# Turning the squared distances into weights: pairs of blocks with two exponentials and one subtraction

## The chip, the cores and the metric

The kernel runs on all 8 cores of one Trainium2 chip. Each core works alone on half of one batch element's queries (2048 of 4096 tokens) against all 4096 keys; the cores exchange nothing. The metric is the device time of the slowest core. Before the change it is 4728.23 us, the median of three runs (4728.14 to 4728.63).

## The reference, cut to what matters

One layer: a layer norm, attention with a kernel of inverse squared distance in place of softmax, a residual, then a second layer norm and a product with the signs of a weight.

```python
P = layernorm(x) @ W_in + b_in           # 16 heads, each Q, K, V, G of 64 columns
d2 = q2[..., :, None] + k2[..., None, :] - 2.0 * qk
W = power(EPS + sqrt(maximum(d2, 0)), -2)          # EPS = 1e-4
W = W / (EPS + sum(W, axis=-1, keepdims=True))
H = G * (W @ V)
x = x + H @ W_out + b_out
x = x + layernorm(x) @ sign(weight).T
```

The matrix W has 4096 x 2048 entries for each head and core; it is never stored, only computed in tiles and contracted with V at once. The power is computed from L = Ln(d2): with d = exp(L/2), (EPS + d)^-2 is close to exp(-L) * (1 - 2 EPS exp(-L/2)).

## The kernel before, in words

Every engine has its own list of steps, written by Python code in the order in which the helper `st` is called for that engine; each step waits for counts of semaphores and then adds to one. Nothing is reordered afterwards, so the order of the emitting code is the order of each engine's queue, and a waiting step holds back everything behind it on its engine. DMAs are issued by SyncE (big loads and stores) and by GpSimd (rows of one partition).

Stages: first layer norm and transposition into `XnT` (some 230 us), the projection of head 0, then the attention loop over 16 heads, then the output projection, the second layer norm and the last product.

The attention loop runs over 1024 regions, r = 0 to 1023: 16 heads, 4 blocks of 512 queries in each, 16 regions in each block. A region is 256 keys by 512 queries. The 64 regions of a head are called slots 0 to 63 below. For one region:

- `emit_S` (L478): two matmuls (512 columns each) write the squared distances to one of two PSUM tiles `pS`; they wait until region r-2 has left it.
- `emit_c12`: ScalarE computes `Lb` = Ln (L490) and `Eb` = Exp(-L/2 + ln 2 EPS) (L495).
- `emit_c3` (L500): VectorE adds the two, in float32, 128 x 1024.
- `emit_c4` (L508): ScalarE computes the weights `wb` = Exp(-(sum)) in bfloat16; four such tiles.
- `emit_A` (L521): two matmuls add weights times V to a PSUM bank `pA`; the 65th row collects the sum of the weights.

The loop writes, at step r: Ln and Exp of r, the addition of r, the distances of r+1, then the last Exp and the matmuls with V of r-1. After the 16th region of a block comes the epilogue (`emit_epilogue`): VectorE copies `pA` to `A_sb` (L534), GpSimd issues a DMA of its sum row (L540), ScalarE takes Ln and Exp of it (L543, L545), VectorE splits it into two bfloat16 rows (L548, L550), TensorE spreads them (L557, L561), and VectorE multiplies (L566 and L574 or L581).

Between these steps `splice` puts the projection of the next head, in 61 groups (the first empty), one after almost every slot: slots 2 to 5 Q, 6 to 13 K (eight matmuls of 512 columns each, L331, and a VectorE copy out of the single PSUM tile `pp`, L341 or L350), slots 14 to 47 V (eight matmuls of 64 columns, L362, a copy L369), 48 to 51 G (as Q, L374), and 52 to 63 the squared norms of K and Q. A group of this last kind, a row group below, is: VectorE squares 512 columns (`KQsq`, L388), TensorE sums over partitions with one matmul (L396), VectorE copies the row out (`k2row`, L400), GpSimd sends it by DMA into `Kaug` or `Qaug` (L405, L410). The first `emit_S` of a head waits for the last of these DMAs. The last head has no such groups. The weights of the next head are loaded and cast after slot 0 (`flush_w`, L312, L316).

Of the kernel before, what the change touches and what calls it, by code (L numbers as in the profile page):

```python
# [34 lines left out]
def build_nc():  # L35
# [448 lines left out]

    def emit_c12(r):
        ps = r % 2
        w = [(s_peS, 2 * r + 2)]
        if r >= 2:
            w.append((s_c3, r - 1))
        st("scalar", lambda e, ps=ps, r=r: e.activation(  # L490
            out=Lb[r % 2][:], in_=pS[ps][:], func=AF.Ln), waits=w, inc=s_c1)
        w = [(s_c1, r + 1)]
        if r >= 2:
            w.append((s_c4, r - 1))
        st("scalar", lambda e, r=r: e.activation(  # L495
            out=Eb[r % 2][:], in_=Lb[r % 2][:], func=AF.Exp, scale=-0.5, bias=LN2EPS),
           waits=w, inc=s_c2)

    def emit_c3(r):
        st("vector", lambda e, r=r: e.tensor_tensor(  # L500
            out=Eb[r % 2][:], in0=Lb[r % 2][:], in1=Eb[r % 2][:], op=ALU.add),
           waits=[(s_c2, r + 1)], inc=s_c3)

    def emit_c4(r):
        w = [(s_c3, r + 1)]
        if r >= 4:
            w.append((s_wcons, 2 * r - 6))
        st("scalar", lambda e, r=r, ws=r % 4: e.activation(  # L508
            out=wb[ws][:], in_=Eb[r % 2][:], func=AF.Exp, scale=-1.0),
           waits=w, inc=s_c4)  # L510
# [390 lines left out]
```

How the kernel before makes its waits and increments, by code:

```python
            def run(eng):  # L840
                for waits, fn, inc, inc_n in steps[name]:
                    for (sm, val) in waits:
                        if val > 0:
                            eng.wait_ge(sm.h, val)
                    inst = fn(eng)
                    if inc is not None:
                        inst.then_inc(inc.h, inc_n)
```

## Time and profile before

| what | value |
|---|---|
| median of three runs | 4728.23 us |
| the profiled execution, own time | 4748.2 us |
| its span (slowest core, first to last instruction) | 4746.6 us |
| spans of the eight cores | 4719.4 to 4746.6 us |
| mean granted TensorE clock, of full speed | 0.629 to 0.633 |
| ScalarE busy | 3168.7 us (67%) |
| TensorE matmul busy | 2870.4 us (60%) |
| VectorE busy | 2254.5 us (47%) |
| GpSimd busy | 145.7 us (3%) |
| attention loop, in the span | 373 to 4393 us |

Busy times are of one execution on its slowest core. The engines work side by side, so that their shares do not add up; what a stage costs is read from the work and the waits of that stage. A row of the order of time gives start, duration, engine, line, operation, tiles, and in brackets how long the engine stood idle before it and for whom. Granted clock 0.50 is 1.2 GHz and 1.00 is 2.4 GHz. Durations contain the latency of an instruction, so that two of one engine that do not wait for each other overlap a little; what one costs the engine is the distance of two starts.

### The profile page before, as it was taken

How to read it: one execution, taken by the hardware profiler on the slowest of the kernel's cores; microseconds unless marked ns; L12 is line 12 of the kernel's file. 1: busy time of each engine (PE TensorE's matmuls, PEld its weight loads, DVE VectorE, ACT ScalarE, POOL GpSimd, SP SyncE). 2: the span in 40 equal slices, each digit the busy share in tenths (PEclk: the TensorE clock that was granted, in tenths of full speed). 3: DMA queues.
4: the chain of work that ended last, by engine and by line, in shares of the span. 5: the costliest groups of instructions: out<-in, count | busy, mean ns of one | idle time of the engine just before them, and what ended most of it. 6: DMA issues, size and time to landing. Idle time of an engine off the chain costs nothing.

```text
span 4746.6 us, 50533 instructions; the slowest of 8 cores (4719.4 to 4746.6 us)
## 1 busy us (share of the span) xinstructions
PE 2870.4 (60%) x11472; PEld 1018.3 (21%) x11472; DVE 2254.5 (47%) x3142; ACT 3168.7 (67%) x3345; POOL 145.7 (3%) x300
## 2 busy tenths in 40 slices
PE   1146666666666576666666666666565766655626
PEld 0122222121212121222222121212121212211202
DVE  4524444545444454454544445454444544533254
ACT  2206868687868687777878686868686877888000
POOL 0000000000000000000000000000000000000000
PEclk9986565656566565656565656565665656555656
DMA  2200000000000000000000000000000000000301
GB/s 76 69 10 10 1 10 2 10 1 10 2 11 1 10 2 5 6 1 10 2 10 1 10 2 10 1 10 2 11 1 10 2 1 17 1 1 2 120 14 71
DMA packets 41423, 64.47 MB, mean 14 GB/s; under 512 B 12992, under 2 KB 29376, under 8 KB 40128
## 3 DMA queue, kind: packets, MB, share of 16 engines
q1 hardware_dynamic: 31680, 58.79, 3.9%
q0 software_dynamic: 9472, 2.45, 0.3%
q8 instruction: 123, 2.02, 0.2%
q14 instruction: 148, 1.21, 0.1%
HBM read 50.39 MB, written 8.39 MB: 12 GB/s over the span
## 4 chain that ended last, share of the span: by engine, by line
issue 29%; ACT 27%; PE 22%; DVE 14%; DMA 6%; ACTq 1%; DVEq 1%; SPq 0%; POOLq 0%
ACT Lb L490 14%; ACT wb L508 9%; PE pp L331 6%; PE pA L521 4%; PE pS L478 3%; DVE k2row L400 3%; PE pp L396 2%; DMA Wst<-w_in 2%; DMA rsrow<-A_sb 2%; DVE KQsq L388 2%; PE pS L815 1%; PE pS L663 1%; ACT Eb L495 1%; ACTq L844 1%; PE pp L362 1%
## 5 line engine op out<-in xcount | busy, mean ns | idle before, releaser
L500 DVE TENSOR_TENSOR Eb<-Lb,Eb 128x1024 f32<-128x1024 f32 x1024 | 1251.5, 1223 | 472.0 <-ACT Eb L495 415.8
L521 PE MATMUL pA<-wb,Vs 128*65 128x512 bf16 x2048 | 943.7, 558 | 790.9 <-ACT wb L508 785.0
L490 ACT ACTIVATE Lb<-pS 128x1024 f32<-128x1024 f32 x1024 | 1035.0, 1011 | 468.7 <-PE pS L478 466.3
L495 ACT ACTIVATE Eb<-Lb 128x1024 f32<-128x1024 f32 x1024 | 1082.1, 1057 | 154.7 <-ACT Lb L490 6.9
L508 ACT ACTIVATE wb<-Eb 128x1024 bf16<-128x1024 f32 x1024 | 1065.3, 1040 | 141.4 <-DVE Eb L500 140.6
L478 PE MATMUL pS<-Qaug,Kaug 66*128 66x512 bf16 x2048 | 944.0, 560 | 57.2 <-POOLq L416 56.8
L521 PEld LDWEIGHTS pA<-wb,Vs 128*65 128x65 bf16 x2048 | 257.5, 127 | 1541.8 <-issue 1529.3
L331 PE MATMUL pp<-XnT,Wbf 128*64 128x512 bf16 x2048 | 543.6, 413 | 40.3 <-DVE Wbf L316 25.0
L369 DVE CAST Vs<-pp 128x64 bf16<-128x64 f32 x512 | 114.7, 224 | 557.0 <-PE pp L362 556.9
L362 PEld LDWEIGHTS pp<-Wbf,XnT 128*128 128x128 bf16 x4096 | 281.5, 129 | 257.5 <-issue 254.7
L362 PE MATMUL pp<-Wbf,XnT 128*128 128x64 bf16 x4096 | 313.5, 240 | 16.4 <-DVE Vs L369 15.4
L331 PEld LDWEIGHTS pp<-XnT,Wbf 128*64 128x64 bf16 x2048 | 219.2, 117 | 334.4 <-issue 193.2
L557 PE MATMUL pA<-rnhl,ones_rowb 1*64 1x512 bf16 x64 | 38.4, 600 | 400.5 <-DVE rnhl L550 400.5
L478 PEld LDWEIGHTS pS<-Qaug,Kaug 66*128 66x128 bf16 x2048 | 177.6, 121 | 311.0 <-issue 308.8
L543 ACT ACTIVATE rlrow<-rsrow 1x512 f32<-1x512 f32 x64 | 40.2, 628 | 285.2 <-DMA rsrow<-A_sb 285.2
L400 DVE CAST k2row<-pp 1x512 bf16<-1x512 f32 x192 | 130.4, 679 | 190.4 <-PE pp L396 190.4
L350 DVE TENSOR_SCALAR Kaug<-pp,bin_sb 64x512 bf16<-64x512 f32 x128 | 95.5, 746 | 167.3 <-PE pp L331 167.3
L396 PE MATMUL pp<-KQsq,ones_col 64*1 64x512 bf16 x128 | 70.8, 553 | 138.9 <-DVE KQsq L388 138.9
L224 PE MATMUL pT<-c_identb,xnf 128*128 128x128 bf16 x256 | 32.4, 306 | 199.4 <-DVE xnf L212 199.4
L548 DVE CAST rnhl<-rnrow 1x512 bf16<-1x512 f32 x64 | 26.6, 416 | 243.2 <-ACT rnrow L545 243.2
L540 POOL DMA_DIRECT2D rsrow<-A_sb x64 | 31.2, 488 | 2857.5 <-DVE A_sb L534 2807.0
L188 ACT ACTIVATE sqscr<-xst 128x1024 f32<-128x1024 f32 x32 | 33.8, 1056 | 126.7 <-DVE lnrows L185 126.7
(85 smaller groups left out, 1256.2 us busy)
## 6 DMA issues: line engine op xcount, KB each, us to landing
xst<-x SPq DMA_DIRECT2D x32, 512.0 KB, 3.7
Wst<-w_in SPq DMA_DIRECT2D x128, 128.0 KB, 2.1
XT<-xT SPq DMA_DIRECT2D x8, 1024.0 KB, 17.2
...
xst<-w_out SPq DMA_DIRECT2D x8, 512.0 KB, 4.6
xst<-w_ffn SPq DMA_DIRECT2D x8, 512.0 KB, 3.5
Kaug<-k2row POOLq DMA_DIRECT2D x128, 1.0 KB, 1.5
...
```

The lines of the kernel that those rows point to most:

```text
L331: return e.matmul(pp[0:64, :], Wbf[hb][:, c * 256 + cols0:c * 256 + cols0 + 64], XnT[:, c * SLEN + n * 512:c * SLEN + (n + 1) * 512], star ...
L350: return e.tensor_scalar(out=Kaug[hb][0:64, n * 512:(n + 1) * 512], in0=pp[0:64, :], scalar1=bin_sb[64:128, 2 * h:2 * h + 1], scalar2=None ...
L362: return e.matmul(pp[0:128, 0:64], XnT[:, c * SLEN + t * 128:c * SLEN + (t + 1) * 128], Wbf[hb][:, c * 256 + 128:c * 256 + 192], start=(c ...
L369: return e.tensor_copy(out=Vs[hb][:, t * 65:t * 65 + 64], in_=pp[0:128, 0:64])
L396: return e.matmul(pp[0:1, :], scol[0:64, :], KQsq[sl][:], start=True, stop=True)
L400: return e.tensor_copy(out=k2row[sl][:], in_=pp[0:1, :])
L478: st("tensor", lambda e, hb=hb, qc=qc, stile=stile, ps=ps, k=k: e.matmul(pS[ps][:, k * 512:(k + 1) * 512], Kaug[hb][:, stile * 128:(stile ...
L490: st("scalar", lambda e, ps=ps, r=r: e.activation(out=Lb[r % 2][:], in_=pS[ps][:], func=AF.Ln), waits=w, inc=s_c1)
L495: st("scalar", lambda e, r=r: e.activation(out=Eb[r % 2][:], in_=Lb[r % 2][:], func=AF.Exp, scale=-0.5, bias=LN2EPS), waits=w, inc=s_c2)
L500: st("vector", lambda e, r=r: e.tensor_tensor(out=Eb[r % 2][:], in0=Lb[r % 2][:], in1=Eb[r % 2][:], op=ALU.add), waits=[(s_c2, r + 1)], in ...
L508: st("scalar", lambda e, r=r, ws=r % 4: e.activation(out=wb[ws][:], in_=Eb[r % 2][:], func=AF.Exp, scale=-1.0), waits=w, inc=s_c4)
L521: st("tensor", lambda e, hb=hb, stile=stile, ws=r % 4, k=k, bk=bk: e.matmul(pAb[bk][0:65, :], Vs[hb][:, stile * 65:stile * 65 + 65], wb[ws ...
```

## The change

Two regions, 2s and 2s+1, are now handled together after their logarithms. The logarithm stays one instruction for each region, and writes one half of a tile `Lb` of 2048 columns. After the second, ScalarE computes `Ea` = Exp(-L) in float32 and `Ebc` = Exp(-1.5 L + ln 2 EPS) in bfloat16, 2048 columns each (`emit_c24`), and VectorE subtracts them into `wb`, bfloat16, 128 x 2048 (`emit_c3`). So three exponential-type passes over each element stay three, but the last step before the matmuls is now on VectorE, and the addition and last exponential are gone. There is one `Ea` and one `Ebc`, and two `wb` of double size: the first exponential of a pair waits for the subtraction of the pair before. The matmuls with V of a pair come together, four in a row, one step later, and the epilogue behind them. Larger tiles need room: the tiles `xst` and `sqscr` are given back after the first layer norm, and the later stages get their own (`wst2`, `wst3`, `sq2`); the first loads of the output weight now wait for the last distance matmul, those of the last weight for the end of the output projection.

```diff
-    Lb = [salloc(f"Lb{i}", [128, 1024], F32, side="right") for i in range(2)]
-    Eb = [salloc(f"Eb{i}", [128, 1024], F32, side="right") for i in range(2)]
-    wb = [salloc(f"wb{i}", [128, 1024], BF16, side="right") for i in range(4)]
+    Lb = [salloc(f"Lb{i}", [128, 2048], F32, side="right") for i in range(2)]
+    Ea = salloc("Ea0", [128, 2048], F32, side="right")
+    Ebc = salloc("Ebc", [128, 2048], BF16, side="right")
+    wb = [salloc(f"wb{i}", [128, 2048], BF16, side="right") for i in range(2)]
...
+    def emit_c1(r):
         ps = r % 2
+        st("scalar", lambda e, ps=ps, sb=(r // 2) % 2, half=r % 2: e.activation(
+            out=Lb[sb][:, half * 1024:half * 1024 + 1024],
+            in_=pS[ps][:], func=AF.Ln),
+           waits=[(s_peS, 2 * r + 2)], inc=s_c1)
+
+    def emit_c24(s):
+        st("scalar", lambda e, s=s: e.activation(
+            out=Ea[:], in_=Lb[s % 2][:], func=AF.Exp, scale=-1.0),
+           waits=[(s_c1, 2 * s + 2), (s_c3, s)], inc=s_c2)
+        st("scalar", lambda e, s=s: e.activation(
+            out=Ebc[:], in_=Lb[s % 2][:], func=AF.Exp, scale=-1.5, bias=LN2EPS),
+           waits=[], inc=s_c2)
+
+    def emit_c3(s):
+        st("vector", lambda e, s=s: e.tensor_tensor(
+            out=wb[s % 2][:], in0=Ea[:], in1=Ebc[:], op=ALU.subtract),
+           waits=[(s_c2, 2 * s + 2), (s_wcons, max(0, 4 * s - 4))], inc=s_c3)
...
-            w = [(s_c4, r + 1)]
+            w = [(s_c3, s + 1)]
...
-        emit_c12(r)
-        emit_c3(r)
+        emit_c1(r)
+        if r % 2 == 1:
+            emit_c24(r // 2)
+            emit_c3(r // 2)
         nxt_head_start = (r + 1) % (NQC * NREG) == 0
         if r + 1 < NTOT and not nxt_head_start:
             emit_S(r + 1)
-        if r >= 1:
-            emit_c4(r - 1)
-            emit_A(r - 1)
-            hh, qq, gg = rinfo(r - 1)
+        if r % 2 == 0 and r >= 2:
+            s = r // 2
+            emit_A(2 * s - 2)
+            emit_A(2 * s - 1)
+            hh, qq, gg = rinfo(2 * s - 1)
             if gg == NREG - 1:
-                emit_epilogue(r - 1)
+                emit_epilogue(2 * s - 1)
...
-           waits=[(s_xfree[sl], NST // 2), (s_wo, max(0, s_wo.n - 1))], inc=s_xld[sl], inc_n=16)
+           waits=[(s_peS, s_peS.n), (s_wo, max(0, s_wo.n - 1))], inc=s_xld[sl], inc_n=16)
...
-           waits=[(s_sg, max(0, s_sg.n - 1)), (s_wo, WO_DONE)], inc=s_xld[sl], inc_n=16)
+           waits=[(s_sg, max(0, s_sg.n - 1)), (s_x1, X1_DONE)], inc=s_xld[sl], inc_n=16)
```

ScalarE's queue around an epilogue (rlrow and rnrow), in the kernel before:

```order
L490 ACTIVATE Lb0<-pS0 128x1024
L495 ACTIVATE Eb0<-Lb0 128x1024
L508 ACTIVATE wb3<-Eb1 128x1024
L543 ACTIVATE rlrow<-rsrow 1x512
L545 ACTIVATE rnrow<-rlrow 1x512
L490 ACTIVATE Lb1<-pS1 128x1024
L495 ACTIVATE Eb1<-Lb1 128x1024
L508 ACTIVATE wb0<-Eb0 128x1024
L490 ACTIVATE Lb0<-pS0 128x1024
```

and in the changed kernel:

```order
L488 ACTIVATE Lb1<-pS0 128x1024
L488 ACTIVATE Lb1<-pS1 128x1024
L494 ACTIVATE Ea0<-Lb1 128x2048
L497 ACTIVATE Ebc<-Lb1 128x2048
L488 ACTIVATE Lb0<-pS0 128x1024
L538 ACTIVATE rlrow<-rsrow 1x512
L540 ACTIVATE rnrow<-rlrow 1x512
L488 ACTIVATE Lb0<-pS1 128x1024
L494 ACTIVATE Ea0<-Lb0 128x2048
L497 ACTIVATE Ebc<-Lb0 128x2048
```

Before, the exponential that feeds the block's last matmuls stands directly ahead of rlrow; now only a logarithm stands between the last pair's exponentials and rlrow.

TensorE's queue where the row groups are spliced in (pS are distances, pA the matmuls with V, pp a row group's matmul), before:

```order
L396 MATMUL pp<-KQsq1,ones_col 1x512
L478 MATMUL pS0<-Qaug0,Kaug0 128x512 x2
L521 MATMUL pA2<-wb0,Vs0 65x512 x2
L396 MATMUL pp<-KQsq0,ones_col 1x512
L478 MATMUL pS1<-Qaug0,Kaug0 128x512 x2
L521 MATMUL pA2<-wb1,Vs0 65x512 x2
L396 MATMUL pp<-KQsq1,ones_col 1x512
L478 MATMUL pS0<-Qaug0,Kaug0 128x512 x2
L521 MATMUL pA2<-wb2,Vs0 65x512 x2
```

and changed:

```order
L479 MATMUL pS0<-Qaug0,Kaug0 128x512 x2
L397 MATMUL pp<-KQsq0,ones_col 1x512
L479 MATMUL pS1<-Qaug0,Kaug0 128x512 x2
L516 MATMUL pA2<-wb0,Vs0 65x512 x4
L397 MATMUL pp<-KQsq1,ones_col 1x512
L479 MATMUL pS0<-Qaug0,Kaug0 128x512 x2
L397 MATMUL pp<-KQsq0,ones_col 1x512
L479 MATMUL pS1<-Qaug0,Kaug0 128x512 x2
L516 MATMUL pA2<-wb1,Vs0 65x512 x4
L397 MATMUL pp<-KQsq1,ones_col 1x512
```

Each row group still stands ahead of the next distance matmuls; the four matmuls with V come after every second one.

VectorE's queue at the same place (Eb or wb is the addition or subtraction, KQsq and k2row the row group), before:

```order
L388 TENSOR_TENSOR KQsq1<-Kaug1 64x512
L400 CAST k2row1<-pp 1x512
L300 NO_OP
L500 TENSOR_TENSOR Eb1<-Lb1,Eb1 128x1024
L388 TENSOR_TENSOR KQsq0<-Kaug1 64x512
L400 CAST k2row0<-pp 1x512
L300 NO_OP
L500 TENSOR_TENSOR Eb0<-Lb0,Eb0 128x1024
L388 TENSOR_TENSOR KQsq1<-Kaug1 64x512
L400 CAST k2row1<-pp 1x512
```

and changed:

```order
L401 CAST k2row1<-pp 1x512
L301 NO_OP
L502 TENSOR_TENSOR wb0<-Ea0,Ebc 128x2048
L389 TENSOR_TENSOR KQsq0<-Kaug1 64x512
L401 CAST k2row0<-pp 1x512
L301 NO_OP
L389 TENSOR_TENSOR KQsq1<-Kaug1 64x512
L401 CAST k2row1<-pp 1x512
L301 NO_OP
```

Two row groups now follow each other between two subtractions, and the first of them stands behind a subtraction of 2048 columns, where every one stood behind an addition of 1024.

## Rows read from the trace of the kernel before

**Rows 1.** The page: its head, and busy us and share of the span.
```profile
span 4746.6 us, 50533 instructions; the slowest of 8 cores (4719.4 to 4746.6 us)
...
PE 2870.4 (60%) x11472; PEld 1018.3 (21%) x11472; DVE 2254.5 (47%) x3142; ACT 3168.7 (67%) x3345; POOL 145.7 (3%) x300
```

**Rows 2.** Stretches: Q/K, V, row groups, head boundary (length; busy us (count); PEclk, DMA, GB/s).
```profile
1418.24:1431.19 12.95, 11.96 (x49) 4.51 (x49) 7.89 (x8) 11.95 (x13) 0.00 (x0) 1.00 0.00 1
1466.88:1503.60 36.72, 27.35 (x136) 11.04 (x136) 17.18 (x24) 34.96 (x37) 0.00 (x0) 0.50 0.00 0
1592.76:1613.81 21.05, 15.28 (x31) 2.79 (x31) 13.39 (x19) 18.17 (x19) 2.90 (x6) 0.50 0.01 1
1620.82:1661.76 40.94, 15.95 (x42) 4.53 (x41) 14.32 (x23) 16.42 (x18) 1.45 (x3) 0.55 0.09 26
```

**Rows 3.** Groups by line and shape: busy us, mean ns of one, idle before.
```profile
L550 DVE TENSOR_TENSOR rnhl<-rnrow,rnhl 1x512 bf16<-1x512 f32 x64 | 43.5, 679 | 6.6
...
L543 ACT ACTIVATE rlrow<-rsrow 1x512 f32<-1x512 f32 x64 | 40.2, 628 | 285.2 <-DMA rsrow<-A_sb 285.2
```

**Rows 4.** Order of time, V stretch: start, duration, engine, line.
```profile
1473.00 1.00 ACT L490 ACTIVATE Lb<-pS 128x1024 f32<-128x1024 f32 x1
...
1473.24 1.03 PE L521 MATMUL pA<-wb,Vs 128*65 128x512 bf16 x2 [1.17 <-ACT wb L508]
...
1474.15 1.06 ACT L495 ACTIVATE Eb<-Lb 128x1024 f32<-128x1024 f32 x1
...
1474.51 1.04 PE L478 MATMUL pS<-Qaug,Kaug 66*128 66x512 bf16 x2
...
1475.11 1.04 ACT L508 ACTIVATE wb<-Eb 128x1024 bf16<-128x1024 f32 x1
...
1475.31 1.23 DVE L500 TENSOR_TENSOR Eb<-Lb,Eb 128x1024 f32<-128x1024 f32 x1 [0.28 <-ACT Eb L495]
```

**Rows 5.** Order of time, K stretch, TensorE at full clock.
```profile
1422.84 1.91 PE L331 MATMUL pp<-XnT,Wbf 128*64 128x512 bf16 x8
...
1424.69 0.60 PE L478 MATMUL pS<-Qaug,Kaug 66*128 66x512 bf16 x2
...
1424.87 0.75 DVE L350 TENSOR_SCALAR Kaug<-pp,bin_sb 64x512 bf16<-64x512 f32 x1 [1.38 <-PE pp L331]
...
1425.45 1.02 ACT L490 ACTIVATE Lb<-pS 128x1024 f32<-128x1024 f32 x1 [0.21 <-PE pS L478]
```

**Rows 6.** Order of time, row groups.
```profile
1592.76 1.23 DVE L500 TENSOR_TENSOR Eb<-Lb,Eb 128x1024 f32<-128x1024 f32 x1 [0.27 <-DVE k2row L400]
...
1593.90 0.41 DVE L388 TENSOR_TENSOR KQsq<-Kaug 64x512 bf16<-64x512 bf16 x1
...
1594.57 0.58 PE L396 MATMUL pp<-KQsq,ones_col 64*1 64x512 bf16 x1 [0.96 <-DVE KQsq L388]
...
1595.08 1.04 PE L478 MATMUL pS<-Qaug,Kaug 66*128 66x512 bf16 x2
...
1595.32 0.68 DVE L400 CAST k2row<-pp 1x512 bf16<-1x512 f32 x1 [1.01 <-PE pp L396]
...
1596.27 1.02 ACT L490 ACTIVATE Lb<-pS 128x1024 f32<-128x1024 f32 x1 [0.33 <-PE pS L478]
```

**Rows 7.** Order of time, epilogue in the V stretch.
```profile
1503.84 1.03 PE L521 MATMUL pA<-wb,Vs 128*65 128x512 bf16 x2 [0.75 <-ACT wb L508]
...
1505.12 0.75 DVE L534 TENSOR_SCALAR A_sb<-pA,ebv 65x512 f32<-65x512 f32 x1 [1.04 <-PE pA L521]
...
1508.08 0.63 ACT L543 ACTIVATE rlrow<-rsrow 1x512 f32<-1x512 f32 x1 [4.38 <-DMA rsrow<-A_sb]
...
1509.34 1.00 ACT L490 ACTIVATE Lb<-pS 128x1024 f32<-128x1024 f32 x1
...
1513.62 1.02 ACT L490 ACTIVATE Lb<-pS 128x1024 f32<-128x1024 f32 x1 [1.14 <-PE pS L478]
```

**Rows 8.** The page, DMA issues: KB each, us to landing.
```profile
xst<-w_ffn SPq DMA_DIRECT2D x8, 512.0 KB, 3.5
```

More of the change, by code:

```diff
@@ L89, in build_nc @@
     lnrows = salloc("lnrows", [128, 8], F32)
-    sqscr = salloc("sqscr", [128, D], F32)
-    xst = [salloc(f"xst{i}", [128, D], F32) for i in range(2)]
+    sqscr = salloc("sqscr", [128, D], F32, side="right")
+    xst = [salloc(f"xst{i}", [128, D], F32, side="right") for i in range(2)]
     XnT = salloc("XnT", [128, NCH * SLEN], BF16)
@@ L237, in build_nc @@
     LN1_XNT = s_xnt.n
-    sfree("xnf1", "xnf0")
+    sfree("xnf1", "xnf0", "xst1", "xst0", "sqscr")
     sfree("pT1", "pT0")
@@ L483, in emit_S @@
                waits=w, inc=s_peS)
-    def emit_c12(r):
+    def emit_c1(r):
         ps = r % 2
[L487 to L510, printed above, removed]
+        st("scalar", lambda e, ps=ps, sb=(r // 2) % 2, half=r % 2: e.activation(
[13 more added lines that the diff above has]
+           waits=[(s_c2, 2 * s + 2), (s_wcons, max(0, 4 * s - 4))], inc=s_c3)
     def emit_A(r):
@@ L515, in emit_A @@
         bk = (h * NQC + qc) % 2
+        s = r // 2
         for k in range(2):
             stile = 2 * g + k
-            w = [(s_c4, r + 1)]
+            w = [(s_c3, s + 1)]
             if stile == 0:
                 w.append((s_epi, prev_e4b[bk]))
-            st("tensor", lambda e, hb=hb, stile=stile, ws=r % 4, k=k, bk=bk: e.matmul(
+            st("tensor", lambda e, hb=hb, stile=stile, ws=s % 2, half=r % 2, k=k, bk=bk: e.matmul(
                 pAb[bk][0:65, :],
                 Vs[hb][:, stile * 65:stile * 65 + 65],
-                wb[ws][:, k * 512:(k + 1) * 512],
+                wb[ws][:, half * 1024 + k * 512:half * 1024 + (k + 1) * 512],
                 start=(stile == 0), stop=(stile == NST - 1)),
@@ L605, in build_nc @@
             emit_S(r + 1)
-        if r >= 1:
-            emit_c4(r - 1)
-            emit_A(r - 1)
-            hh, qq, gg = rinfo(r - 1)
+        if r % 2 == 0 and r >= 2:
+            s = r // 2
+            emit_A(2 * s - 2)
+            emit_A(2 * s - 1)
+            hh, qq, gg = rinfo(2 * s - 1)
             if gg == NREG - 1:
-                emit_epilogue(r - 1)
+                emit_epilogue(2 * s - 1)
         slot_in_head = r % (NQC * NREG)
@@ L617, in build_nc @@
             emit_S(r + 1)
-    emit_c4(NTOT - 1)
+    emit_A(NTOT - 2)
     emit_A(NTOT - 1)
@@ L627, in build_nc @@
     sfree("Htmp", "T1b", "rnhl", "rnrow", "rlrow", "rsrow", "A_sb1", "A_sb0",
-          "wb3", "wb2", "wb1", "wb0", "Eb1", "Eb0", "Lb1", "Lb0",
+          "wb1", "wb0", "Ebc", "Ea0", "Lb1", "Lb0",
           "k2row1", "k2row0", "KQsq1", "KQsq0", "ebv",
@@ L633, in build_nc @@
     sfree("pA2", "pA")
+    wst2 = [salloc(f"wst2_{i}", [128, D], F32, side="right") for i in range(2)]
     Wout_bf = salloc("Wout_bf", [128, 8 * D], BF16, side="right")
@@ L640, in build_nc @@
         sl = c % 2
-        st("sync", lambda e, c=c, sl=sl: e.dma_start(out=xst[sl][:], in_=wout_h[c * 128:(c + 1) * 128, :]),
-           waits=[(s_xfree[sl], NST // 2), (s_wo, max(0, s_wo.n - 1))], inc=s_xld[sl], inc_n=16)
+        st("sync", lambda e, c=c, sl=sl: e.dma_start(out=wst2[sl][:], in_=wout_h[c * 128:(c + 1) * 128, :]),
+           waits=[(s_peS, s_peS.n), (s_wo, max(0, s_wo.n - 1))], inc=s_xld[sl], inc_n=16)
         st("vector", lambda e, c=c, sl=sl: e.tensor_copy(out=Wout_bf[:, c * 1024:(c + 1) * 1024],
-                                                         in_=xst[sl][:]),
+                                                         in_=wst2[sl][:]),
            waits=[(s_xld[sl], s_xld[sl].n), (s_epi, ATT_EPI)], inc=s_wo)
@@ L676, in build_nc @@
     X1_DONE = s_x1.n
-    sfree("Wout_bf")
+    sfree("Wout_bf", "wst2_1", "wst2_0")
     sfree("H7", "H6", "H5", "H4", "H3", "H2", "H1", "H0")
     signWT = salloc("signWT", [128, 8 * D], BF16, side="right")
+    wst3 = [salloc(f"wst3_{i}", [128, D], F32, side="right") for i in range(2)]
+    sq2 = salloc("sq2", [128, 512], F32, side="right")
     x1n_bf = salloc("x1n_bf", [128, NCH * TOWN], BF16, side="right")
@@ L693, in build_nc @@
         sl = oc % 2
-        st("sync", lambda e, oc=oc, sl=sl: e.dma_start(out=xst[sl][:], in_=wffn_h[oc * 128:(oc + 1) * 128, :]),
-           waits=[(s_sg, max(0, s_sg.n - 1)), (s_wo, WO_DONE)], inc=s_xld[sl], inc_n=16)
-        st("scalar", lambda e, sl=sl: e.activation(out=sgb[:], in_=xst[sl][:], func=AF.Sign),
+        st("sync", lambda e, oc=oc, sl=sl: e.dma_start(out=wst3[sl][:], in_=wffn_h[oc * 128:(oc + 1) * 128, :]),
+           waits=[(s_sg, max(0, s_sg.n - 1)), (s_x1, X1_DONE)], inc=s_xld[sl], inc_n=16)
+        st("scalar", lambda e, sl=sl: e.activation(out=sgb[:], in_=wst3[sl][:], func=AF.Sign),
            waits=[(s_xld[sl], s_xld[sl].n), (s_ptf, s_ptf.n),
@@ L795, in build_nc @@
             st("vector", lambda e, a0=a0, a1_=a1_: e.tensor_tensor(
-                out=sqscr[:, 0:512], in0=x1T[:, a0:a1_], in1=pA_ln2[:, 0:512], op=ALU.mult),
+                out=sq2[:, 0:512], in0=x1T[:, a0:a1_], in1=pA_ln2[:, 0:512], op=ALU.mult),
                waits=[(s_ab, abn), (s_x1n, s_x1n.n)], inc=s_x1n)
             st("vector", lambda e, a0=a0, a1_=a1_: e.tensor_tensor(
-                out=x1n_bf[:, a0:a1_], in0=sqscr[:, 0:512], in1=pS[0][:, 0:512], op=ALU.add),
+                out=x1n_bf[:, a0:a1_], in0=sq2[:, 0:512], in1=pS[0][:, 0:512], op=ALU.add),
                waits=[(s_x1n, s_x1n.n)], inc=s_x1n)
```

## The prediction

> **What bounds the kernel now.** I read the page first: the span is 4746.6 us and ScalarE, busiest, has 3168.7 us or 67% [rows 1]. That alone would make ScalarE's work the price of everything, so next I cut the attention loop into stretches by what is spliced in, as a head repeats the same four [rows 2]. In the V stretch twelve regions take 36.72 us, 3.06 us each, with ScalarE busy 34.96 us: here ScalarE is the bound, at granted clock 0.50. In the K stretch four regions take 12.95 us, 3.24 each, at clock 1.00, with TensorE and ScalarE both full. In the row-group stretch six regions take 21.05 us, 3.51 each, and ScalarE is busy 18.17 only: something else sets the pace. The head boundary takes 40.94 us from the addition of slot 63 to the matmuls of slot 3, with ScalarE busy 16.42.
>
> The order of time shows why. In the V stretch ScalarE's starts are 1.15 us apart after a Ln (the Exp waits for its result) and 0.96 after an Exp: 1473.00, 1474.15, 1475.11 [rows 4]. In the row stretch the loop is closed on VectorE: addition at 1592.76, KQsq 1.14 later, its matmul 0.67 later, k2row 0.75 later, and the next addition behind it [rows 6]; 21.05/6 = 3.51 is this loop. At a block's end ScalarE stands still while the sum row goes through VectorE and a DMA: A_sb at 1505.12, rlrow at 1508.08 with 4.38 us idle before it [rows 7].
>
> As a check I add up a head: 14 slots of Q, K and G outside the boundary at 3.24 (45.3), 34 of V at 3.06 (104.0), 12 of rows at 3.51 (42.1), the boundary 40.9, and three epilogues at some 7.1 us over the steady pace (below): 253.6. The loop takes 4020 us, the last head without groups four blocks of some 56; the 15 others are left with 253 each. So the pieces hold.
>
> **The new step on its own.** A logarithm of 1024 columns is unchanged. An Exp of 1024 columns lasts 1.06 us [rows 4] and a function of 512 columns 0.628 [rows 3], so 0.43 us for each 512 columns: 2048 columns last 1.91 us, and cost ScalarE 0.96 + 0.85 = 1.81 from start to start. Six instructions of 6.12 us for two regions become four of 0.95 + 1.15 + 1.81 + 1.81 = 5.72. That is the 0.40 us for each pair that can be won, and all of it.
>
> The Trainium skill, page "VectorE: DVE Perf Modes", section on the TRN2 errata, gives ScalarE a fixed cost of 224 cycles for each operation on SBUF. By it two operations less would save an estimated 0.37 us where the starts in the V stretch, 0.96 us apart for 0.85 us of columns, show 0.1 us each as long as nothing waits. By that rule ScalarE's four would take about 5.4 us. It changes nothing where the subtraction decides, next.
>
> The subtraction has 2048 columns. No row of before has this shape. Addition 1.23 us for 1024 columns [rows 4, 6]; a two-input operation with one float32 and one bfloat16 input and bfloat16 out takes 0.679 us for 512 [rows 3], on the same line (1.23 - 0.68 = 0.55 for 512), so mixed types run no faster. 2048 columns: 1.23 + 2 x 0.54 = 2.31 us. Bounds: 1.23 (were the bfloat16 side to double the rate) and 2.5. I take 2.31, as the row with the same types lies on that line.
>
> **V stretch.** The new first exponential waits for the subtraction of the pair before, because there is one `Ea`. Loop: release 0.15 (between 0.10, Exp end 1475.21 to addition 1475.31 [rows 4], and 0.26, KQsq end to matmul [rows 6]), Ea 1.81, Ebc 1.90 to its end, 0.10 release, subtraction 2.31: 6.27 us. The two logarithms lie beside the subtraction and need only 2.0. TensorE's chain fits beside it: from the subtraction's end 0.25 + four V matmuls 1.7 + V group and distances up to the second pair of distances, in all 3.7, its result 1.18 later [S to Ln in rows 6], 4.9; the logarithm may start as late as 5.2. So 6.27 against 6.12: +0.15 us for each pair, 17 pairs in a head: +2.6 us.
>
> **Q, K and G stretches.** At clock 1.00 the group's matmuls take 1.85 us up to the next distances, its copy starts 2.03 after the group and lasts 0.75, and Ln can start 0.76 after the distances [rows 5]. New, from the first of four V matmuls: group at 0.95 (four times 512 columns at 2.4 GHz and 0.1), copy 2.98 to 3.72, distances 2.80, second group at 3.95 (one `pp`), second distances 5.80, Ln 6.55, and Ea at 7.7. The subtraction before it ends at 6.07. The first pair thus repeats after 6.32 us, the next waits for that late Ln and takes 7.74: mean 7.03 against 6.48. +0.55 for 7 pairs: +3.9 us.
>
> **Row stretch, the largest term.** VectorE's order is subtraction, KQsq, k2row, KQsq, k2row; TensorE's first row matmul stands ahead of the distances of slot 2s+3. So from a subtraction's start: KQsq at 2.31 - 0.08 = 2.23, its matmul +0.67, distances +0.51, Ln +1.19 [rows 6], Ea +1.15 [rows 4], Ebc +1.81, its end +1.90, release 0.10: the next subtraction at 9.56 us. Before, two regions took 7.02. +2.54 for the five pairs from slots 52/53 to 62/63: +12.7 us in each of 15 heads, and +0.5 for the entry. Ahead of it nothing hides: ScalarE stands idle from the first Ln to the second. The V matmuls and the second row group (done at about 7.4) lie inside.
>
> **Epilogues.** From the last subtraction's start: V matmuls at 2.56, A_sb at 4.69 (1.28 after the first of two matmuls [rows 7], plus 0.85 for two more at 1.2 GHz), rlrow 2.96 later at 7.65, Ln 1.26 later at 8.91 [rows 7], Ea 10.05, subtraction 13.86; the second Ln is held by the V copy behind it, and the second subtraction starts at 20.5. Two steady pairs are 12.5, so an epilogue costs 8.0. Before it cost some 7.1: from the V matmuls to the second Ln after it 9.78 us [rows 7], where the steady pace has 2.8 (1473.24 to the second start of Ln after it, one period of 3.06 less 0.24) [rows 4]. +0.85, three in a head inside the stretches: +2.5. One more Ln is hidden in the wait; that is counted.
>
> **Head boundary.** The same waits in the same order (row DMA, distances, V matmuls, sum row, weight casts): worked the same way it comes to about 41 against 40.94 [rows 2]. I take 0, bounds -1 and +2.
>
> **Outside the loop.** Loads of the last weight start only when the output projection ends: one landing of 3.5 us [rows 8] is exposed, +4. The output weight's first loads still land before the last epilogue: 0. The other stages keep their work.
>
> **Sum.** A head: 2.6 + 3.9 + 13.2 + 2.5 = 22.2, x 15 = 333; the last head, without groups, 32 x 0.15 + 4 x 0.6 = 7; outside 4: +344 us. The profiled execution's own time is 4748.2 us, 0.4% above the median of the runs; 4748 + 344 = 5092 there, 4728 + 344 = 5072 as a median.
>
> **The rivals.** (1) The clock falls in the Q, K and G stretches. There TensorE streams for 5.1 us of each 6.48 now at clock 1.00, and would for 5.1 of 7.03, with a gap of up to 1.5 us before the V matmuls; in the V stretch, at 2.1 of 3.06 us at 0.50, it does not rise [rows 2]. At 1.2 GHz the pair costs 10.3 (columns alone: 24 matmuls of 0.427). If it stayed down, +3.3 x 7 x 15 = 343; since a dense TensorE brought the clock up before, half of it: 172 more, 5245. The Trainium skill, page "TensorE: Matmul & The Clock Gate", section on HAM oscillation, says idle gaps between groups throw the clock back and forth; the rows can't tell whether these gaps do. (2) The row stretch does not lengthen, because the second Ln's distances are there in time. Against it: the printed order. Without that term, 5072 - 198 = 4874. (3) Faster: ScalarE's work decides. Place: the wait of Ea for the subtraction. It needs that to last under 1.75 us (2.0 less the two releases). Then the V stretch wins 0.40 a pair, and with the same in every pair of the loop 512 x 0.40 = 205 us are won: 4523; with the row stretch still at 9.56 - 1.07 = 8.5 it is about 4725, no change. For it: only the bfloat16 side; against it, the 0.679 us row [rows 3].
>
> **How the numbers follow.** Forecast 0.66; its own range 4990 to 5140 (boundary, epilogues, releases). Clock 0.18, row stretch unlengthened 0.08, ScalarE decides 0.06 (half of it no change), other 0.02 slower. The range 4900 to 5250 leaves out most of (3), part of (2) and the worst of (1). A measurement of this kernel tells 0.2%, 9 us, from no change. Slower 0.94, same 0.03, faster 0.03.
>
> **What would show it.** Subtraction near 2.31 us; in the V stretch Ea idle about 0.4 to 0.5 us for VectorE, a pair in 6.27; in the row stretch subtractions 9.56 us apart and the second Ln idle some 3.5 us for distances; rlrow idle about 6.8 us instead of 4.4; clock 1.00 in the K stretch with pairs of 6.3 and 7.7 in turn. A subtraction of 1.2 us, or row pairs at 7, would prove it wrong.

## The result, and the profile after

The changed kernel takes 5043.41 us (median of 8 runs, 5040.2 to 5050.34) against 4729.29 us for the kernel before (8 runs): a ratio of 1.0657, 95% interval 1.0641 to 1.0672, 314 us slower. The forecast was 5072 us, 344 us slower, range 4900 to 5250.

The page of the changed kernel, its head, the line of busy times and five of the costliest groups, in the columns of [rows 1] and [rows 3]:

```profile
span 5042.4 us, 44906 instructions; the slowest of 8 cores (5037.1 to 5042.4 us)
...
PE 2717.7 (54%) x11472; PEld 1043.6 (21%) x11472; DVE 2170.8 (43%) x2630; ACT 3015.4 (60%) x2321; POOL 145.6 (3%) x300
...
L502 DVE TENSOR_TENSOR wb<-Ea,Ebc 128x2048 bf16<-128x2048 f32 x512 | 1173.4, 2292 | 742.9 <-ACT Ebc L497 734.0
L488 ACT ACTIVATE Lb<-pS 128x1024 f32<-128x1024 f32 x1024 | 1020.7, 1012 | 766.7 <-PE pS L479 764.4
...
L494 ACT ACTIVATE Ea<-Lb 128x2048 f32<-128x2048 f32 x512 | 977.8, 1910 | 339.2 <-DVE wb L502 302.1
L497 ACT ACTIVATE Ebc<-Lb 128x2048 bf16<-128x2048 f32 x512 | 969.1, 1893 | 0.0
...
L538 ACT ACTIVATE rlrow<-rsrow 1x512 f32<-1x512 f32 x64 | 40.2, 628 | 407.6 <-DMA rsrow<-A_sb 407.6
```

Each engine does less or the same: ScalarE 3015 us where it had 3169, VectorE 2171 where it had 2255 [rows 1]. The time went into waits. The Ln (L488) stands idle 767 us, nearly all of it for the distances from TensorE; in the kernel before that wait came to 466 us:

```profile
L490 ACT ACTIVATE Lb<-pS 128x1024 f32<-128x1024 f32 x1024 | 1035.0, 1011 | 468.7 <-PE pS L478 466.3
```

The first exponential (L494) has a new wait of 302 us for the subtraction. And rlrow (L538) stands 408 us for its DMA, where it had 285 [rows 3].

The same four kinds of stretch as in [rows 2], here V (six pairs), row groups (five), K/Q (four) and the head boundary (columns: stretch, length, busy us and count by engine, granted clock, DMA):

```profile
1873.96:1911.55 37.59, 24.56 (x138) 11.29 (x136) 15.69 (x18) 33.40 (x25) 0.00 (x0) 0.59 0.00 1
1941.56:1989.40 47.84, 22.71 (x48) 5.59 (x48) 21.98 (x25) 28.05 (x20) 4.85 (x10) 0.50 0.01 1
2035.08:2062.85 27.77, 23.14 (x98) 8.92 (x96) 15.05 (x13) 22.58 (x17) 0.00 (x0) 1.00 0.00 1
1989.40:2029.77 40.37, 15.07 (x39) 4.84 (x40) 14.35 (x20) 13.45 (x11) 1.50 (x3) 0.54 0.09 28
```

| stretch | before, two slots | after, a pair | forecast |
|---|---|---|---|
| V, clock 0.50 before | 6.12 | 37.59 / 6 = 6.27 | 6.27 |
| Q/K, clock 1.00 | 6.48 | 27.77 / 4 = 6.94 | 7.03 |
| row groups, clock 0.50 | 7.02 | 47.84 / 5 = 9.57 | 9.56 |
| head boundary | 40.94 | 40.37 | about 41 |

From one block sum at a head's start to the next, the DMAs of the sum row are 252.4 us apart before (1633.89 to 1886.26) and 272.8 after (1728.74 to 2001.58): 20.5 us a head.

In the V stretch, in order of time (start, duration, engine, line, what it was idle for):

```profile
1880.22 2.29 DVE L502 TENSOR_TENSOR wb<-Ea,Ebc 128x2048 bf16<-128x2048 f32 x1 [1.18 <-ACT Ebc L497]
...
1882.61 1.91 ACT L494 ACTIVATE Ea<-Lb 128x2048 f32<-128x2048 f32 x1 [0.73 <-DVE wb L502]
...
1882.66 1.70 PE L516 MATMUL pA<-wb,Vs 128*65 128x512 bf16 x4 [2.43 <-DVE wb L502]
...
1884.42 1.89 ACT L497 ACTIVATE Ebc<-Lb 128x2048 bf16<-128x2048 f32 x1
...
1886.22 1.92 ACT L488 ACTIVATE Lb<-pS 128x1024 f32<-128x1024 f32 x2
1886.49 2.29 DVE L502 TENSOR_TENSOR wb<-Ea,Ebc 128x2048 bf16<-128x2048 f32 x1 [1.37 <-ACT Ebc L497]
```

The subtraction starts at 1880.22, ends at 1882.51, and Ea follows 0.10 later after 0.73 us of idleness. Ebc and two Ln follow, the Ln beside the next subtraction, and the round closes in 6.27 us.

In the row stretch:

```profile
1960.44 1.00 ACT L488 ACTIVATE Lb<-pS 128x1024 f32<-128x1024 f32 x1
1960.70 2.29 DVE L502 TENSOR_TENSOR wb<-Ea,Ebc 128x2048 bf16<-128x2048 f32 x1 [2.07 <-ACT Ebc L497]
1962.91 0.41 DVE L389 TENSOR_TENSOR KQsq<-Kaug 64x512 bf16<-64x512 bf16 x1
...
1963.57 0.58 PE L397 MATMUL pp<-KQsq,ones_col 64*1 64x512 bf16 x1 [4.83 <-DVE KQsq L389]
...
1964.09 1.04 PE L479 MATMUL pS<-Qaug,Kaug 66*128 66x512 bf16 x2
...
1964.91 1.91 PE L516 MATMUL pA<-wb,Vs 128*65 128x512 bf16 x4
...
1965.22 1.02 ACT L488 ACTIVATE Lb<-pS 128x1024 f32<-128x1024 f32 x1 [3.78 <-PE pS L479]
...
1966.39 1.91 ACT L494 ACTIVATE Ea<-Lb 128x2048 f32<-128x2048 f32 x1
...
1968.20 1.89 ACT L497 ACTIVATE Ebc<-Lb 128x2048 bf16<-128x2048 f32 x1
...
1970.27 2.29 DVE L502 TENSOR_TENSOR wb<-Ea,Ebc 128x2048 bf16<-128x2048 f32 x1 [2.07 <-ACT Ebc L497]
```

Each link of the forecast chain can be read off: subtraction, KQsq 2.21 later, its matmul 0.66, distances 0.52, and the second Ln at 1965.22 after 3.78 us of idleness for them; Ea and Ebc behind it; next subtraction 9.57 us after the first. The first Ln had run at 1960.44 and gained nothing by it.

At a block's end:

```profile
1853.85 2.29 DVE L502 TENSOR_TENSOR wb<-Ea,Ebc 128x2048 bf16<-128x2048 f32 x1 [1.18 <-ACT Ebc L497]
...
1856.29 1.89 PE L516 MATMUL pA<-wb,Vs 128*65 128x512 bf16 x4 [1.82 <-DVE wb L502]
...
1858.42 0.75 DVE L529 TENSOR_SCALAR A_sb<-pA,ebv 65x512 f32<-65x512 f32 x1 [2.15 <-PE pA L516]
...
1861.38 0.63 ACT L538 ACTIVATE rlrow<-rsrow 1x512 f32<-1x512 f32 x1 [6.79 <-DMA rsrow<-A_sb]
...
1862.64 1.00 ACT L488 ACTIVATE Lb<-pS 128x1024 f32<-128x1024 f32 x1
```

Rlrow stands idle 6.79 us where it stood 4.38 [rows 7]: between the last exponentials and the sum row now lie the subtraction and four V matmuls instead of two.

### The profile page after: what moved, and what is told of

It is laid out like the page before. It is cut to its first block, busy times and chain, and to the rows that moved or that the text cites. A ratio compares the mean times of both kernels' runs of the same rounds, so it can differ in the third digit from the quotient of the medians.

```text
span 5042.4 us, 44906 instructions; the slowest of 8 cores (5037.1 to 5042.4 us)
## 1 busy us (share of the span) xinstructions
PE 2717.7 (54%) x11472; PEld 1043.6 (21%) x11472; DVE 2170.8 (43%) x2630; ACT 3015.4 (60%) x2321; POOL 145.6 (3%) x300
## 4 chain that ended last, share of the span: by engine, by line
ACT 37%; DVE 25%; PE 20%; issue 11%; DMA 6%; DVEq 1%; ACTq 0%; SPq 0%; POOLq 0%
ACT Ea L494 16%; DVE wb L502 16%; ACT Ebc L497 15%; PE pp L332 7%; PE pA L516 4%; ACT Lb L488 3%; PE pS L479 3%; DMA Wst<-w_in 2%; DMA rsrow<-A_sb 2%; PE pp L397 1%; PE pS L816 1%; PE pS L662 1%; DVE A_sb L529 1%; DVE KQsq L389 1%; DVEq L845 1%
## 5 line engine op out<-in xcount | busy, mean ns | idle before, releaser
L502 DVE TENSOR_TENSOR wb<-Ea,Ebc 128x2048 bf16<-128x2048 f32 x512 | 1173.4, 2292 | 742.9 <-ACT Ebc L497 734.0
L488 ACT ACTIVATE Lb<-pS 128x1024 f32<-128x1024 f32 x1024 | 1020.7, 1012 | 766.7 <-PE pS L479 764.4
L516 PE MATMUL pA<-wb,Vs 128*65 128x512 bf16 x2048 | 835.0, 552 | 895.0 <-DVE wb L502 894.9
L494 ACT ACTIVATE Ea<-Lb 128x2048 f32<-128x2048 f32 x512 | 977.8, 1910 | 339.2 <-DVE wb L502 302.1
L497 ACT ACTIVATE Ebc<-Lb 128x2048 bf16<-128x2048 f32 x512 | 969.1, 1893 | 0.0
L479 PE MATMUL pS<-Qaug,Kaug 66*128 66x512 bf16 x2048 | 912.4, 549 | 56.9 <-POOLq L417 56.5
L516 PEld LDWEIGHTS pA<-wb,Vs 128*65 128x65 bf16 x2048 | 294.1, 144 | 1413.5 <-issue 1384.5
L538 ACT ACTIVATE rlrow<-rsrow 1x512 f32<-1x512 f32 x64 | 40.2, 628 | 407.6 <-DMA rsrow<-A_sb 407.6
L529 DVE TENSOR_SCALAR A_sb<-pA,ebv 65x512 f32<-65x512 f32 x64 | 47.8, 747 | 203.5 <-PE pA L516 203.5
L397 PE MATMUL pp<-KQsq,q_col 64*1 64x512 bf16 x64 | 37.2, 582 | 166.7 <-DVE KQsq L389 166.7
```

The lines of the kernel that those rows point to most:

```text
L397: return e.matmul(pp[0:1, :], scol[0:64, :], KQsq[sl][:], start=True, stop=True)
L479: st("tensor", lambda e, hb=hb, qc=qc, stile=stile, ps=ps, k=k: e.matmul(pS[ps][:, k * 512:(k + 1) * 512], Kaug[hb][:, stile * 128:(stile ...
L488: st("scalar", lambda e, ps=ps, sb=(r // 2) % 2, half=r % 2: e.activation(out=Lb[sb][:, half * 1024:half * 1024 + 1024], in_=pS[ps][:], fu ...
L494: st("scalar", lambda e, s=s: e.activation(out=Ea[:], in_=Lb[s % 2][:], func=AF.Exp, scale=-1.0), waits=[(s_c1, 2 * s + 2), (s_c3, s)], in ...
L497: st("scalar", lambda e, s=s: e.activation(out=Ebc[:], in_=Lb[s % 2][:], func=AF.Exp, scale=-1.5, bias=LN2EPS), waits=[], inc=s_c2)
L502: st("vector", lambda e, s=s: e.tensor_tensor(out=wb[s % 2][:], in0=Ea[:], in1=Ebc[:], op=ALU.subtract), waits=[(s_c2, 2 * s + 2), (s_wcon ...
```

## The experiments

All ran beside the kernel before (medians 4729.0 to 4729.7 us). Ratios are to it, with the 95% interval.

**The row group moved.** Two edits to the order, in the row stretch only:

```diff
...
             s = r // 2
+            if r % (NQC * NREG) > 52:
+                splice(r % (NQC * NREG), NQC * NREG)
             emit_A(2 * s - 2)
...
-        splice(slot_in_head + 1, NQC * NREG)
+        if not (slot_in_head > 52 and slot_in_head % 2 == 1) or nxt_head_start:
+            splice(slot_in_head + 1, NQC * NREG)
```

> Changed kernel, but in the row stretch the row group of an odd slot is emitted one step later, behind the second distance matmuls of the next pair and ahead of its four V matmuls. Theory (the row stretch's 9.57 us a pair come from the subtraction standing ahead of the row group, and the row group's matmul ahead of the distances that the second Ln waits for): a pair falls to about 6.8 us, 5 pairs x 15 heads x 2.75 = 207 us less, so about 4836 us. Rival (the row stretch is held by VectorE's amount of work or by the row DMAs, wherever the group stands): within 20 us of 5043.

Measured 4847.46 us, 1.0247 (1.0230 to 1.0264): 196 us less than the changed kernel. Row stretch of this run:

```profile
1878.10:1913.18 35.08, 22.06 (x46) 5.25 (x46) 21.98 (x26) 27.95 (x20) 4.37 (x9) 0.53 0.01 1
```

Five pairs in 35.08 us, 7.02 each (about 6.8 was expected). The two regions cost what they cost before the change. So the place of the row group in the queues made this term, not the amount of work: all instructions are still there.

**The subtraction made short.**

```diff
-    Ea = salloc("Ea0", [128, 2048], F32, side="right")
+    Ea = salloc("Ea0", [128, 2048], BF16, side="right")
```

> Changed kernel with Ea in bfloat16, so that the subtraction has only 16-bit operands; everything else is the same (the weights are rounded twice). Theory (the 2.29 us subtraction lies in the loop of every stretch): subtraction about 1.24 us; V stretch 6.27 to 5.72 a pair (17 pairs), Q/K/G 6.94 to 6.5 (7), rows 9.57 to 8.5 (5), each block's end 1.07 shorter (4): 22.5 us a head, in all some 360 us less, about 4684 us, under the kernel before. Rival (ScalarE's passes or TensorE hold the loop and the subtraction is mostly beside them): not under 4980 us.

Measured 4709.98 us, 0.9957 (0.9943 to 0.9972): 333 us less (360 expected), and 0.4% under the kernel before, little, but the interval leaves 1 out. The subtraction's group and three stretches (V, row groups, K):

```profile
L502 DVE TENSOR_TENSOR wb<-Ea,Ebc 128x2048 bf16<-128x2048 bf16 x512 | 627.2, 1225 | 951.6 <-ACT Ebc L497 945.7 <-DVE Wbf L317 5.3
```

```profile
1708.34:1742.41 34.07, 22.07 (x136) 10.30 (x136) 9.39 (x17) 33.19 (x25) 0.00 (x0) 0.69 0.00 0
1823.17:1865.68 42.51, 22.71 (x48) 5.59 (x48) 16.64 (x26) 28.04 (x20) 4.85 (x10) 0.50 0.01 1
1909.12:1934.75 25.63, 23.00 (x98) 9.01 (x96) 10.78 (x13) 22.57 (x17) 0.00 (x0) 1.00 0.00 1
```

1.225 us for the subtraction; pairs of 34.07 / 6 = 5.68, 42.51 / 5 = 8.50 and 25.63 / 4 = 6.41 us, forecast 5.72, 8.5 and 6.5. One operation's 1.07 us is worth 333 us, 0.65 us for each of the 512 pairs, because it lies in the loop of every stretch. One input tile in 16 bits instead of 32 decided the sign of the change.

**Both.**

> Both edits of the two runs above it in this call, the later row group and Ea in bfloat16. If the two terms are separate: 4684 less 75 x (8.5 - 5.8), about 4480 us. If they are the same wait seen twice: no lower than 4640.

Measured 4512.09 us, 0.9538 (0.9524 to 0.9552): 198 less than with the short subtraction alone, against 196 for the row group alone. The terms are separate.

**A second Ea.** In float32, the wait of Ea taken away by a second buffer. `Ebc` stays single, so the wait for the subtraction before goes over to it:

```diff
-    Ea = salloc("Ea0", [128, 2048], F32, side="right")
+    Ea = [salloc(f"Ea{i}", [128, 2048], F32, side="right") for i in range(2)]
...
-            out=Ea[:], in_=Lb[s % 2][:], func=AF.Exp, scale=-1.0),
-           waits=[(s_c1, 2 * s + 2), (s_c3, s)], inc=s_c2)
+            out=Ea[s % 2][:], in_=Lb[s % 2][:], func=AF.Exp, scale=-1.0),
+           waits=[(s_c1, 2 * s + 2), (s_c3, max(0, s - 1))], inc=s_c2)
...
-           waits=[], inc=s_c2)
+           waits=[(s_c3, s)], inc=s_c2)
```

> Changed kernel with a second float32 Ea, so that the first exponential of a pair no longer waits for the subtraction of the pair before (the three rows of the epilogue share one tile to make room; Ebc stays single). Theory (in the V stretch the wait of Ea, 0.73 us a pair, is real, but the second distances of a pair come so late on TensorE that the loop subtraction, V matmuls, distances, Ln, exponentials, subtraction closes at about 12.1 us for two pairs): V stretch 6.27 to 6.05, the last head 5.72, K and row stretches unchanged: 75 us less, 4950 to 4985. Rival (only the single Ea holds the pair): V stretch 5.72, some 160 us less, about 4885.

Measured 4949.72 us, 1.0460 (1.0443 to 1.0478): 94 us less, not 158. In the V stretch seven pairs take 41.90 us, 5.99 each; in the last head, which has no spliced groups, pairs are 5.67 us apart:

```profile
4559.89 2.29 DVE L501 TENSOR_TENSOR wb<-Ea,Ebc 128x2048 bf16<-128x2048 f32 x1 [0.56 <-ACT Ebc L496]
4565.56 2.29 DVE L501 TENSOR_TENSOR wb<-Ea,Ebc 128x2048 bf16<-128x2048 f32 x1 [3.39 <-ACT Ebc L496]
```

So there are two loops behind one another. The wait for Ea is 0.28 us of the 0.60 that a long subtraction costs a pair in the V stretch; behind it stands TensorE with the distances of the second region, for which the Ln stands idle here, as in this row:

```profile
1844.92 1.02 ACT L487 ACTIVATE Lb<-pS 128x1024 f32<-128x1024 f32 x1 [0.50 <-PE pS L478]
```

The new wait of Ebc (115 us in all) falls on the heads' starts, 8.37 us at 1994.44, and not into the V stretch.

**The formula without pairs.** The kernel before, three functions of 1024 columns and a subtraction of 1024, two of each tile:

```diff
...
         st("scalar", lambda e, r=r: e.activation(
-            out=Eb[r % 2][:], in_=Lb[r % 2][:], func=AF.Exp, scale=-0.5, bias=LN2EPS),
-           waits=w, inc=s_c2)
+            out=Eb[r % 2][:], in_=Lb[r % 2][:], func=AF.Exp, scale=-1.0),
+           waits=[(s_c1, r + 1), (s_c3, max(0, r - 1))], inc=s_c2)
+        st("scalar", lambda e, r=r: e.activation(
+            out=Ebc[r % 2][:], in_=Lb[r % 2][:], func=AF.Exp, scale=-1.5, bias=LN2EPS),
+           waits=[], inc=s_c2)
...
-            out=Eb[r % 2][:], in0=Lb[r % 2][:], in1=Eb[r % 2][:], op=ALU.add),
...
+            out=wb[r % 4][:], in0=Eb[r % 2][:], in1=Ebc[r % 2][:], op=ALU.subtract),
+           waits=[(s_c2, 2 * r + 2), (s_wcons, max(0, 2 * r - 6))], inc=s_c3)
...
```

> Kernel before with only the new formula, without pairs: three functions of 1024 columns in one queue (Ln, Exp(-L), Exp(-1.5L+c)), a mixed-type subtraction of 1024 columns, two Ea and two Ebc. Theory (pairing, not the formula, costs): V stretch 3.06 a region, rows 3.51, and each block's end shorter by some 1.6 us, since the last subtraction lies beside the next region's functions: about 4630 us. Rival (the formula costs, because the last step before the V matmuls is on VectorE): slower than 4729, 4800 or more.

Measured 4685.84 us, 0.9907 (0.9892 to 0.9922). The rival is out, the formula alone wins 44 us (some 100 expected), and not where I said. Rlrow stands idle 279.6 us in all, as before (285): on VectorE the block's `A_sb` stands behind the next region's subtraction, which I had overlooked. A gain shows in the K stretch (first line; V and row groups behind it):

```profile
1894.24:1934.16 39.92, 35.20 (x157) 13.74 (x156) 24.39 (x28) 37.84 (x39) 0.00 (x0) 0.95 0.00 0
1700.52:1740.30 39.78, 28.38 (x138) 11.24 (x138) 17.56 (x25) 37.71 (x39) 0.00 (x0) 0.51 0.00 1
1828.38:1857.36 28.98, 19.02 (x40) 4.25 (x38) 17.85 (x24) 24.09 (x24) 3.90 (x8) 0.50 0.01 1
```

13 regions in 39.92 us there, 3.07 against 3.24 before [rows 2]; V is at 3.06 as before, the row groups at 28.98 / 8 = 3.62 a little worse. Over 14 slots and 12 in each of 15 heads that is some 36 us won and 20 lost; where the rest of the 44 us lies is not shown.

**The epilogue deferred.** Its second half (Ln and Exp of the sum row and all behind them) becomes a function that the loop calls two steps later. The weight casts of a head's start go two slots later too, so that they stay behind it; the two moves were not run apart:

```diff
-                emit_epilogue(2 * s - 1)
+                pend.append((r + 2, emit_epilogue(2 * s - 1)))
...
+        if pend and pend[0][0] <= r:
+            pend.pop(0)[1]()
-        if slot_in_head == 0:
+        if slot_in_head == 2:
             flush_w()
```

In the changed kernel, alone:

> Changed kernel with nothing but the second half of the epilogue emitted one pair later. A block's end costs it some 7.6 us over the steady pace; with the sum row out of the way of ScalarE's queue I expect 2.5 to 3: 5 us x 62 less, about 4735. In the kernel before the same deferral won 205 us, of 290 expected, because TensorE then stood before the spreading matmuls and the next Ln came late; if that holds here too, about 4830.

Measured 4723.24 us (10 runs), 0.9983 (0.9970 to 0.9995): 320 us less, on average 5.0 for each of the 64 blocks. ScalarE's groups in this run (the columns of [rows 3]):

```profile
L488 ACT ACTIVATE Lb<-pS 128x1024 f32<-128x1024 f32 x1024 | 1018.7, 1012 | 963.1 <-PE pS L479 961.7
L494 ACT ACTIVATE Ea<-Lb 128x2048 f32<-128x2048 f32 x512 | 977.7, 1910 | 203.0 <-DVE wb L502 164.0
...
L544 ACT ACTIVATE rlrow<-rsrow 1x512 f32<-1x512 f32 x64 | 39.7, 620 | 28.7 <-DMA rsrow<-A_sb 28.7
```

Set beside the changed kernel's, three waits moved: rlrow's for its DMA from 408 to 29, -379; Ea's for the subtraction from 302 to 164, -138; the Ln's for distances from 764 to 962, +197. Together -320, as much as the loop itself became shorter (first to last subtraction, 4309.9 us and 3989.7). The second belongs to the head's start: there VectorE casts the next weights as their DMAs land, with the subtraction behind them in its order, and Ea stood idle 9.95 us, at 2021.08 in the changed kernel. With the casts two slots later this wait of Ea is gone, but most of it comes back on the Ln: Q's first matmuls wait for the casts, and the distances stand behind these matmuls.

```profile
1909.93 3.54 PE L332 MATMUL pp<-XnT,Wbf 128*64 128x512 bf16 x8 [11.95 <-DVE Wbf L317]
...
1914.11 1.02 ACT L488 ACTIVATE Lb<-pS 128x1024 f32<-128x1024 f32 x1 [14.81 <-PE pS L479]
```

From the subtraction of slots 62/63 to that of slots 4/5 this version takes 43.54 us (1878.51 to 1922.05) and the changed kernel 45.68 (1989.40 to 2035.08): 2.1 won. A block inside a head, from sum-row DMA to sum-row DMA, takes 51.60 (1760.67 to 1812.27) and took 57.69 (1802.08 to 1859.77): 6.1 won. So the gain is almost all from the sum row at the ends of blocks inside a head. In the kernel before:

> Kernel before, but the second half of each epilogue (Ln and Exp of the sum row and all after it) is emitted two regions later, with the weight casts at a head's start behind it. Theory (ScalarE stands idle 4.4 us a block for the sum row, plus 1.1 and 0.4 us behind it, only because rlrow is next in its queue): some 4.9 us x 60 less, about 4435. Rival (the wait moves to TensorE, which then stands before the spreading matmuls while the next distances are behind them): less than 120 us won.

Measured 4523.89 us, 0.9561 (0.9541 to 0.9582): 205 us won, between the theory (some 290) and the rival (under 120). First the kernel before, then this run:

```profile
L508 ACT ACTIVATE wb<-Eb 128x1024 bf16<-128x1024 f32 x1024 | 1065.3, 1040 | 141.4 <-DVE Eb L500 140.6
...
L508 ACT ACTIVATE wb<-Eb 128x1024 bf16<-128x1024 f32 x1024 | 1065.9, 1041 | 0.8 <-PE pA L521 0.8
L490 ACT ACTIVATE Lb<-pS 128x1024 f32<-128x1024 f32 x1024 | 1035.6, 1011 | 689.2 <-PE pS L478 687.3 <-issue 0.2
...
L549 ACT ACTIVATE rlrow<-rsrow 1x512 f32<-1x512 f32 x64 | 39.3, 614 | 4.4 <-DMA rsrow<-A_sb 4.4
```

The same three: rlrow from 285 to 4, -281; the second exponential's wait for VectorE (L508), in the kernel before 141 us and there mostly the 9.18 us behind the casts at each head's start (at 1652.03), to nothing, -141; the Ln's for distances from 466 to 687, +221. Together -201. So the edit took away 422 us of waits, and half came back as a later arrival of distances, on the engine where the rival put it; most of that again at the heads' starts: from the addition of slot 62 to that of slot 4 it takes 43.66 us (1556.90 to 1600.56), and took 44.10 (1617.31 to 1661.41). In the changed kernel the same edit took away 517 and gave back 197: its sum row stood behind a longer chain. In the formula without pairs:

> The new formula without pairs (4686 us), and the second half of the epilogue two regions later. In that run A_sb stood behind the next region's subtraction on VectorE, so that the sum row came no sooner than before. Expected: about 4390, 45 us under the kernel before with the same deferral, if the K stretch's 3.06 us a region (3.24 before) is what the formula gives; equal to it if not.

Measured 4480.63 us, 0.9469 (0.9450 to 0.9487): the 43 us between it and the run before it are the formula's 44 again; the level is 90 above what I wrote, for the same reason as in the run before it.

**All together.**

> The version with the later row group and Ea in bfloat16 (4512 us), and the second half of the epilogue one pair later. Same theories: 5 us x 60 less, about 4220; rival: not under 4400.

Measured 4219.86 us, 0.8918 (0.8901 to 0.8934): the fastest, 509 us under the kernel before. Its weights are rounded to bfloat16 once more. In the change's own precision:

> Changed kernel in its own precision (Ea float32) with all three orders of work mended: later row group, two Ea, deferred second half of the epilogue. If the terms are separate: 4950 (two Ea) less 196 (row group) less 200 to 300 (deferral): 4450 to 4550, 4 to 6% under the kernel before. If the terms are one wait seen three times: above 4650.

Measured 4458.70 us, 0.9427 (0.9402 to 0.9453). Terms one by one: 94 + 196 + 320 = 610 us off 5043 would be 4433; 26 us of them are shared, and the run lies where separate terms were expected (4450 to 4550).

## Why the prediction was right, step by step

**The subtraction, 2.31 us.** Measured 2.292. The row of a mixed-type operation on one partition carried over to 128 partitions and 2048 columns; the bound of 1.23 us was the price with both inputs in 16 bits, as the short version showed.

**ScalarE's four instructions, 5.72 us.** Shown by the last head with two Ea and by the short subtraction, 5.67 to 5.68. Two Exp of 0.96 us from start to start became one of 1.81, so a merged instruction saved 0.1 us; with the one wait for a Ln that fell away, 0.19, this makes the 0.40. By the fixed cost in the Trainium skill, "VectorE: DVE Perf Modes", section on the TRN2 errata, a merged instruction would save an estimated 0.19. The 5.4 us that the prediction names by that rule do not follow from it: 6.12 less 0.37 is 5.75, and a total of 5.67 does not decide between 5.75 and 5.72. The distance of two starts does, and shows 0.1.

**V stretch.** 6.27 as forecast, with small errors that cancel: the releases were 0.10 and 0.18 (forecast 0.15 and 0.10), the subtraction 2.29. Ea was idle 0.73 us, not 0.4 to 0.5; 0.15 of it lies between a Ln's end and its exponential in any case (1474.00 to 1474.15 [rows 4]). That the wait of Ea is its first holder is shown by the second Ea; TensorE's chain, which I had put at 4.9 of 5.2 us allowed, holds next, at 5.99 (6.05 was expected of that run).

**Q, K and G.** The forecast had pairs of 6.32 and 7.74 in turn; the subtractions start at 2035.08, 2041.35, 2048.97, 2055.23 and 2062.85, so 6.27, 7.62, 6.26, 7.62. The term was +0.55 a pair and is +0.46. The clock stayed at 1.00: the first rival is out. The oscillation between levels that the Trainium skill, "TensorE: Matmul & The Clock Gate", section on HAM oscillation, warns of did not show in this stretch. In the V stretch the clock rose at times, 0.59 in the six pairs above where it was 0.50 [rows 2], and that won nothing, as ScalarE and VectorE hold that loop.

**Row groups, the largest term.** 9.57, forecast 9.56, and the moved group gave 196 us back. The second rival, that this stretch does not lengthen, is out; it comes true only in the other order.

**Epilogues, the mis-sized term.** +0.85 us each in the forecast. A V block of 16 regions takes 57.7 us (sum-row DMAs at 1802.08 and 1859.77), 50.1 of it at the steady pace, so 7.6 over it. By the same measure it was 7.0 before (DMAs at 1703.00 and 1758.98, 49.0 at the steady pace), where the forecast had 7.1: some +0.55. The chain up to the first subtraction behind the block's last was right, 13.81 us for 13.86. What was too long is the next link: the second subtraction stands at 20.11, not 20.5. The sum of the forecast puts the second Ln 15.5 us after the block's last subtraction; it started after 15.1 (1868.91), the copy of V that it hangs on at 1867.01, and waited 0.50 us. That the epilogue's price as such hangs on rlrow's place in the queue, the deferral showed.

**Head boundary.** 40.4, forecast about 41, counted as no change.

**The sum.** A head measures 20.5 us more, forecast 22.2; the 1.7 are mostly the epilogues (0.9) and K (0.6). Times 15, and some 6 for the last head by the same terms, is 313. Outside the loop 4 us were expected. On core 4 the loop from first to last rlrow is 3945.4 us before and 4257.8 after, +312, and the rest of its span 777.0 and 784.0, +7; the medians differ by 314. Of the 30 us by which the forecast is too high, these 1.7 us a head make 26. (Core 3 of the profiled execution of before, which [rows 1] shows, had a slower output projection, 447 ns a matmul against 398 on core 4 and in the changed kernel; its span alone would make the difference 296.)

**The third rival, ScalarE decides.** Its point was a subtraction under 1.75 us. The short subtraction of 1.23 us passed it, and the V stretch fell to 5.68 as it said; the forecast of "about no change" for that case (4725) is 4710 measured.

Open: the deferral and the later weight casts were not run apart, and the 26 us that the terms share when all are put together were not followed.
